# A recommender tower on one core: the beginning reordered, and TensorE's repeated products paced by issued gathers

## What is computed

```python
e = stack([tbl_f[ids[:, f]] for f in range(39)], axis=1)          # (2048, 39, 16)
xk = e
for W, b in ((w0, b0), (w1, b1), (w2, b2)):                       # S = 128 outputs each
    z = relu(einsum('bhd,bkd,hks->bsd', e, xk, W) + b[None, :, None])
    # layers 0 and 1: the first 64 of z are the next xk, the last 64 go out; layer 2: all go out
z = sum over d of the concatenated outputs                        # (2048, 256)
h = relu([z, dense_ctx] @ W_top1 + b_top1); h = relu(h @ W_top2 + b_top2); y = h @ W_top3
```

## Time and profile before

| | us |
|---|---|
| median of 3 runs | 2478.45 (2478.34 to 2480.01) |
| the profiled execution | 2477.58 |
| its span, first to last instruction | 2475.8 |
| TensorE busy in the span | 2422.1 (98%) |
| VectorE busy | 2211.2 (89%) |
| GpSimd busy | 1948.6 (79%) |
| ScalarE busy | 1724.4 (70%) |

### The profile page before, as it was taken

The page is one execution under the profiler, slowest core; times in us unless marked ns, Lnnn a source line. Parts: engine busy times, 40 slices in busy tenths (PEclk is TensorE's granted clock), DMA queues, the critical chain, the costliest instruction groups (busy, mean ns, idle before and its releaser), DMA issues.

```text
span 2475.8 us, 33269 instructions
## 1 busy us (share of the span) xinstructions
PE 2422.1 (98%) x8854; PEld 1640.9 (66%) x8854; DVE 2211.2 (89%) x1876; ACT 1724.4 (70%) x2185; POOL 1948.6 (79%) x1331
## 2 busy tenths in 40 slices
PE   5999999999999999999999999999999999999989
PEld 2566666666666666666666666666666666666655
DVE  1599999999989999999999999899999999999990
ACT  1677777777767777767777776676777777677663
POOL 6688888888878888888888888788888888865550
PEclk9899999999999999999999999999999999999999
DMA  3778667766856766776686677577668667766830
GB/s 74 157 145 175 141 138 160 158 137 141 175 124 139 174 134 140 163 157 137 144 172 138 139 161 160 121 157 160 137 139 174 145 139 154 164 136 134 171 84 0
DMA packets 214716, 352.60 MB, mean 142 GB/s; under 512 B 34382, under 2 KB 47566, under 8 KB 214588
## 3 DMA queue, kind: packets, MB, share of 16 engines
q1 hardware_dynamic: 194717, 347.07, 65.4%
q0 software_dynamic: 19968, 5.15, 2.1%
HBM read 346.97 MB, written 5.12 MB: 142 GB/s over the span
## 4 chain that ended last, share of the span: by engine, by line
PE 54%; POOL 26%; issue 14%; DVE 4%; ACT 1%; POOLq 0%; DMA 0%; ACTq 0%; DVEq 0%
PE ps L858 20%; POOL Pl L397 11%; POOL emb L391 11%; PE ps L868 11%; PE ps L848 10%; PE ps L836 8%; PE ps L831 2%; POOL dir L426 2%; DVE P L731 1%; DVE ps L731 1%; DVE Pl L736 1%; PE ps L983 1%; POOL sqx L403 1%; PE ps L975 1%; PE ps L824 1%
## 5 line engine op out<-in xcount | busy, mean ns | idle before, releaser
L397 POOL TENSOR_TENSOR Pl<-P,Ph 128x1024 fp32r<-128x1024 f32 x448 | 1074.8, 2399 | 285.3 <-ACT Ph L541 261.5
L858 PE MATMUL ps<-Ph,wh 128*128 128x512 f32 x2048 | 965.2, 471 | 9.9 <-ACT Ph L541 9.9
L541 ACT ACTIVATE Ph<-ps 128x1024 fp32r<-128x1024 f32 x576 | 590.3, 1025 | 406.7 <-DVE ps L731 393.0
L731 DVE TENSOR_TENSOR P<-xb,ps 128x1024 f32<-128x1024 f32 x704 | 853.2, 1212 | 2.8 <-DMA xb<-x_dram 2.8
L736 DVE TENSOR_TENSOR Pl<-ps,Ph 128x1024 fp32r<-128x1024 f32 x576 | 705.1, 1224 | 116.1 <-ACT Ph L541 97.4
L858 PE MATMUL ps<-Ph,wl 128*128 128x512 f32 x1920 | 755.5, 393 | 0.0
L868 PE MATMUL ps<-Pl,wh 128*128 128x512 f32 x2048 | 742.2, 443 | 7.4 <-POOL Pl L397 7.4
L391 POOL DMA_INDIRECT emb<-tbl_in,idx x624 | 600.6, 962 | 170.5 <-issue 145.0
L731 DVE TENSOR_TENSOR ps<-xb,ps 128x1024 f32<-128x1024 f32 x576 | 707.1, 1228 | 28.5 <-issue 9.4
L541 ACT ACTIVATE Ph<-P 128x1024 fp32r<-128x1024 f32 x448 | 473.9, 1058 | 186.1 <-DVE P L731 129.8
L868 PEld LDWEIGHTS ps<-Pl,wh 128*128 128x128 f32 x2048 | 384.3, 188 | 200.0 <-issue 118.2
(11 more groups left out here) (68 smaller groups left out, 857.2 us busy)
## 6 DMA issues: line engine op xcount, KB each, us to landing
xb<-x_dram SPq DMA_DIRECT2D x1280, 256.0 KB
emb<-tbl_in,idx POOLq DMA_INDIRECT x624
x_dram<-rows SPq DMA_DIRECT2D x64, 78.0 KB
xb<-w_in SPq DMA_DIRECT2D x16, 128.0 KB
xb<-wt_in SPq DMA_DIRECT2D x2, 512.0 KB, 4.4
xb<-dense_in SPq DMA_DIRECT2D x1, 768.0 KB, 5.3
wp<-w_in SPq DMA_DIRECT2D x4, 128.0 KB
xb<-w0a_in SPq DMA_DIRECT2D x1, 448.0 KB
```

The source lines that it names most:

```text
L397: pool.tensor_tensor(Pl[:, h_slot(ref, c, k)], P[:, p_slot(ref, c, k)], Ph[:, h_slot(ref, c, k)], ALU.subtract).then_inc(low_pool, 1)
L541: act.activation(Ph[:, h_slot(ref, c, k)], p, ACT.Copy).then_inc(rounded, 1)
L731: dve.tensor_tensor(p, xb[:, x], xk.unsqueeze(1).broadcast_to([128, 2, N]), ALU.mult)\
L858: pe.matmul(z_of(c, k), w[:, q, j, :], Ph[:, h_slot(ref, c, k), j, :], start=k in (L1B, L2) and i + j == 0, stop=False)
```

## The change

- DVE: the low halves `wl` of the weights (L702) and the two copies behind them (L711) leave their place ahead of the gathers' end, and stand behind the embedding's low part. What needs them, `transposes(1)` on PE, waits for them (`weights_made` 8). PE's and SP's first waits are for five preparations of weights. `w_st` moves to the end of `xb`, so that the first spreads do not overwrite it.
- The embedding of tile 0 is prepared in two parts: the first four columns d (`D0`) get their high, full and low parts first, and PE's first transposes wait for those alone; the other twelve (`D1`) follow, with their full part on DVE as a `tensor_copy`.
- In the first chunk ACT copies `x2` first and the rows second; PE's first two sums wait for `x2` alone.
- Bias and relu of the lower half (`lower`) of the first chunk's layer 0 and of the last chunk's layer 1 are done by DVE, beside ACT's `direct0` and `direct1`; ACT then copies the result to the upper half.
- The 36 repeated products on PE wait, three at a time, for a count `issued`, which POOL raises after every third gather of tile 0.
- POOL issues 11 gathers of tile 1, not 14, before its first `low`, and 7 behind it.

```diff
--- before.py
+++ after.py
@@ -34,7 +34,7 @@
 
 
 PRE = 4
-WARM = 36
+PACE = 3
 L1B, L2, STEPS = PAIRS - PRE, PAIRS, 2 * PAIRS
 KIND = "GVPVGPVGVPVGVGVGVGVP"
 SPL = [k for k in range(STEPS) if KIND[k] != "P"]
@@ -59,6 +59,7 @@
 SINGLE_STEPS = [k for k in range(STEPS) if TURN[k % PAIRS] == SINGLE // 2]
 assert all(k in SPL for k in SINGLE_STEPS)
 CHUNKS = TILES * CPT
+D0, D1 = slice(0, DC), slice(DC, D)
 NEXT_IDS_AT = (2, 0)
...
@@ -185,6 +186,9 @@
         sel = sel0[0:R2, 0:T0 * R0].rearrange("p (t r) -> p t r", r=R0)
         sel0_st, inc = stage(R2, T0, R0), stage(R0, T0, NF)
         w0a_st, w0b_st = stage(R0, T0, S), stage(R0, T0, S)
+        assert at[0] + NS * 2 * S <= XSLOTS * 2 * N
+        at[0] = XSLOTS * 2 * N - NS * 2 * S
+        assert at[0] >= 2 * PRE * 2 * N
         w_st = stage(128, NS, 2 * S).rearrange("p q (j m) -> p q j m", j=2)
 
         xt = xb[:, :, :, :].rearrange("p q j n -> p (q j) n")
...
@@ -329,8 +338,8 @@
                         .then_inc(xb_in[q], 16)
 
 
-            sp.wait_ge(weights_made, 8)
-            sp.wait_ge(parts_made, 2)
+            sp.wait_ge(weights_made, 5)
+            sp.wait_ge(parts_made, 3)
             write_rows(0, 0)
             for p in range(PRE):
                 spread(0, p)
@@ -434,6 +443,8 @@
             take_ids(0)
             for f in range(NF):
                 gather(f)
+                if f % PACE == PACE - 1:
+                    pool.sem_inc(issued, 1)
 
             def next_ids(T):
 
@@ -442,7 +453,7 @@
                 take_ids(T)
 
             next_ids(1)
-            early, early2 = 14, 18
+            early, early2 = 11, 18
             for f in range(early):
                 gather(f)
             for k in range(L1B, L2):
@@ -556,9 +567,18 @@
                 act.activation(dir1[:, COL1[c % CPT], :], z2_ps, ACT.Relu, bias=bias[:, 2:3]).then_inc(z2_read, 1)
 
 
-            high_emb(0)
-            full_emb(0)
-            copy_x(0, 0)
+            def part(x, d):
+                return x[:, :, d].rearrange("p f d -> p d f")
+
+            act.wait_ge(gathered, 16 * NF)
+            act.activation(emb_h[:, :, D0], emb[:, :, D0], ACT.Copy).then_inc(first_high, 1)
+            act.activation(emb2[:, D0, 0, :], part(emb, D0), ACT.Copy).then_inc(first_full, 1)
+            act.activation(emb_h[:, :, D1], emb[:, :, D1], ACT.Copy).then_inc(emb_high, 1)
+            act.wait_ge(aux_ready, 1)
+            act.activation(x2[:, :], aux_ps[0:R2], ACT.Copy).then_inc(first_x, 1)
+            act.activation(rows_sb, aux_ps[0:NF], ACT.Copy).then_inc(rows_ready, 1)
+            act.wait_ge(rows_ready, 1)
+            act.sem_inc(aux_read, 1)
             square(0, 2, 0, early_ps[0][1])
             rest_squares(0, 0, 1, early_ps[0][0])
             for t in range(1, FULL0):
@@ -566,9 +586,8 @@
             act.wait_ge(squares_done, 1)
             direct0(0)
             act.wait_ge(z0_read, 1)
-            upper(0, z0_ps[:, 0], xk1_upper)
             act.wait_ge(xk1_upper, 1)
-            lower(0, z0_ps[:, 0], xk1_ready)
+            act.activation(z0_ps[hi, 0], z0_ps[lo, 0], ACT.Copy).then_inc(xk1_ready, 1)
 
             act.wait_ge(rows_written, 16)
             copy_x(0, AUX)
@@ -632,9 +651,13 @@
                             direct1(c)
                         if k == RELU1_AT:
                             act.wait_ge(z1_read, T * CPT + c + 1)
-                            upper(1, z1_ps[:, c % 2], xk2_upper)
-                            act.wait_ge(xk2_upper, T * CPT + c + 1)
-                            lower(1, z1_ps[:, c % 2], xk2_ready)
+                            if end:
+                                act.wait_ge(xk2_upper, CHUNKS)
+                                act.activation(z1_ps[hi, c % 2], z1_ps[lo, c % 2], ACT.Copy).then_inc(xk2_ready, 1)
+                            else:
+                                upper(1, z1_ps[:, c % 2], xk2_upper)
+                                act.wait_ge(xk2_upper, T * CPT + c + 1)
+                                lower(1, z1_ps[:, c % 2], xk2_ready)
                         if KIND[k] != "P" and (CPT * ref + c, k) in STEPSET:
                             round_(T, ref, c, k)
                         if end and k == L1B:
@@ -698,17 +721,9 @@
             dve.wait_ge(weights_made, 1)
             dve.tensor_scalar(w0[:, :, :], w0a_st[:, 0:FULL0], 0.5, None, ALU.mult).then_inc(weights_made, 1)
             dve.tensor_scalar(w0b_st[:, FULL0], w0a_st[:, FULL0], 0.5, None, ALU.mult).then_inc(weights_made, 1)
-            dve.wait_ge(parts_made, 2)
-            dve.tensor_tensor(wl[:, :, :, :], w_st, wh[:, :, :, :], ALU.subtract).then_inc(weights_made, 1)
-
             dve.wait_ge(parts_made, 3)
             part = slice(GAP, GAP + REST)
             dve.tensor_tensor(w0x[part, :], w0b_st[part, FULL0], w0x[part, :], ALU.subtract).then_inc(weights_made, 1)
-
-            dve.wait_ge(weights_made, 5)
-            for k in SINGLE_STEPS:
-                q = SPL.index(k)
-                dve.tensor_copy(wh[K1:, q, 1, :], wl[K1:, q, 1, :]).then_inc(weights_made, 1)
 
             dve.wait_ge(incident, 1)
             dve.scalar_tensor_tensor(out=w0[0:NF, 0, :], in0=aux_ps[0:NF, 0:S], scalar=-0.5, in1=w0a_st[0:NF, 0, :],
@@ -742,9 +757,24 @@
                 dve.wait_ge(rest_square, chunk + 1)
                 dve.tensor_tensor(sqx[LOWS, :], rest_sq, sqx[LOWS, :], ALU.subtract).then_inc(rest_ready, 1)
 
+            def lower(layer, z, made):
+                dve.tensor_scalar(z, z, bias[lo, layer:layer + 1], 0.0, ALU.add, ALU.max).then_inc(made, 1)
+
+            def part(x, d):
+                return x[:, :, d].rearrange("p f d -> p d f")
+
+            dve.wait_ge(first_high, 1)
+            dve.tensor_tensor(emb2[:, D0, 1, :], part(emb, D0), part(emb_h, D0), ALU.subtract).then_inc(first_low, 1)
             dve.wait_ge(emb_high, 1)
-            dve.tensor_tensor(emb2[:, :, 1, :], emb[:, :, :].rearrange("p f d -> p d f"),
-                              emb_h[:, :, :].rearrange("p f d -> p d f"), ALU.subtract).then_inc(emb_low, 1)
+            dve.tensor_tensor(emb2[:, D1, 1, :], part(emb, D1), part(emb_h, D1), ALU.subtract).then_inc(emb_low, 1)
+            dve.tensor_copy(emb2[:, D1, 0, :], part(emb, D1)).then_inc(emb_full, 1)
+            dve.wait_ge(parts_made, 2)
+            dve.tensor_tensor(wl[:, :, :, :], w_st, wh[:, :, :, :], ALU.subtract).then_inc(weights_made, 1)
+            dve.wait_ge(weights_made, 6)
+            for k in SINGLE_STEPS:
+                q = SPL.index(k)
+                dve.tensor_copy(wh[K1:, q, 1, :], wl[K1:, q, 1, :]).then_inc(weights_made, 1)
+
             def low_weights():
                 dve.wait_ge(mlp_high, 1)
                 r = slice(2 * GAP, DX)
@@ -755,6 +785,8 @@
                         .then_inc(mlp_low, 1)
 
             rest_low(0)
+            dve.wait_ge(squares_done, 1)
+            lower(0, z0_ps[lo, 0], xk1_upper)
             dve.wait_ge(xk1_ready, 1)
             waiting = None
             for s in range(PRE):
@@ -779,6 +811,9 @@
                                 waiting = None
                             if k == L2 - 1:
                                 low_weights()
+                                dve.wait_ge(plain_done, PLAINS[CHUNKS - 1, L1B - 1])
+                                dve.wait_ge(split_done, SPLITS[CHUNKS - 1, L1B - 1])
+                                lower(1, z1_ps[lo, (CPT - 1) % 2], xk2_upper)
                             continue
                         if k == L1B:
                             dve.wait_ge(xk1_ready, T * CPT + c + 2)
@@ -893,20 +928,31 @@
                 m = pe.matmul(aux_ps[0:NF, 0:S], inc[rows, t, :], w0a_st[rows, t, :], start=t == 0, stop=t == T0 - 1)
             m.then_inc(incident, 1)
 
-            for i in range(WARM):
+            for i in range(PACE, NF):
+                if i % PACE == 0:
+                    pe.wait_ge(issued, i // PACE)
                 pe.matmul(z1_ps[:, 0], wp[:, 0, 0, :], wp[:, 0:2].rearrange("p q j m -> p (q j m)"), start=True, stop=True)
 
 
-            pe.wait_ge(weights_made, 8)
+            pe.wait_ge(weights_made, 5)
             pe.wait_ge(parts_made, 1)
             pe.wait_ge(idx_ready, 2)
-            pe.wait_ge(emb_full, 1)
-            pe.wait_ge(emb_low, 1)
+            pe.wait_ge(first_full, 1)
+            pe.wait_ge(first_low, 1)
             late = None
             for g in range(2):
+                if g:
+                    pe.wait_ge(weights_made, 8)
+                    pe.wait_ge(emb_full, 1)
+                    pe.wait_ge(emb_low, 1)
                 transposes(g)
-                pe.wait_ge(aux_read, READS * g + 1)
+                if g:
+                    pe.wait_ge(aux_read, READS + 1)
+                else:
+                    pe.wait_ge(first_x, 1)
                 for i, t in enumerate((FULL0, 0, 1)):
+                    if i == 2 and not g:
+                        pe.wait_ge(aux_read, 1)
                     sums(t, early_ps[g][i])
```

(5 more changed lines are left out.)

## The result

The changed kernel took 2482.32 us (median of 22 runs, 2478.42 to 2486.76), the kernel before 2478.62 in as many runs beside it: ratio 1.0017, 95% interval 1.0011 to 1.0023. That is no gain but a loss of 3.7 us: less than the 5.0 us (0.2%) that the prediction counted as no change, yet clear of the noise, and far outside the predicted 2467.6 to 2475.3. The profiled execution took 2482.29, its span is 2480.5.

What follows compares the result with a forecast made beforehand. TensorE, busy 98%, was taken as the bound, its start set by the gathers and embedding before about 65 us. Gains 3.34 + 1.28 + 0.61 + 0.68 + 0.67 = 6.6 gave a forecast of 2471.4, range 2467.6 to 2475.3.

Steps and rivals of the forecast that it cites:

- Part 1: Weights' low halves behind tile 0's gathers: the 5.03 gather's stall goes, less 0.55 for increments; net gain 3.34 us.
- The copy was held: POOL's index copy of tile 1 waits for VectorE's subtraction L702 until 64.4; POOL's second subtraction just fits, cost zero.
- Part 2: Between the gathers' landing and the first transposes: preparing a quarter of the embedding first takes 0.90, gaining 1.28 us.
- Part 3: First chunk, x2 copied ahead of the rows: sums start earlier, gain 0.61 us; the later transfers stay hidden.
- Part 4: Lower half on VectorE beside direct0 and direct1: gain 0.68 us in the first chunk, 0.67 in the last.
- The clock: Rival, chance 0.17: shorter TensorE pauses move three steps to full clock, 3 us more gained, 2468.4.
- Part 5: Pacing the 36 repeated products ahead of the first transposes: they end near 54.5, pause about 3.3; priced at 0.
- The slow one: Rival, chance 0.05: each of 12 POOL increments waits for its gather's landing, 1.34 each, 16 in all: 2486.8.
- The stall: Rival, chance 0.05: something else slows the fourteenth gather, which still costs 5.03; part 1 becomes -0.55: 2474.8.
- POOL was not late: Rival, chance 0.09: held copy and slower gathers make POOL's second subtraction 1 to 3 late: 2473.5.

Runs made afterwards that it cites:

- j1: The changed kernel itself, unedited, run again on chip 10 against the kernel before: 2469.75 us, ratio 0.9968.
- j2: The changed kernel without pacing (POOL's increments, TensorE's waits) and with 24 repeated products instead of 36, on chip 10: 2471.25 us, ratio 0.9972.
- h3: The changed kernel without pacing, plus three VectorE operations of 128x1024 at the moved subtraction's old place, on chip 15: 2470.11 us in one run.
- j3: The same kernel as h3, on chip 10 against the kernel before: 2470.82 us, ratio 0.9970.
- i4: The same kernel as h3, timed in several rounds on chip 2 against the kernel before: 2483.27 us, ratio 1.0021.

## Why the prediction was wrong, point by point

The sum itself can be read where the stretch is absent. j1's median is 7.85 under that of before on its chip (2477.6), where 6.6 was forecast (7.1 between medians). The interval of its ratio goes from 4.7 to 10.9 us and holds both.

- *Part 1.* Right in after and j1: the last gather ends at 55.13 and 55.08 for 55.6. The difference is about the increments, priced at 0.55 and free. The copy was held as said, for 4.21 and 4.22 in place of 0.22, and ended at 63.5 and 63.6 (64.4 predicted). The Trainium skill (SBUF — State Buffer, SBUF: two separate sides) says that whichever of the two engines starts first has the shared ports for its whole instruction. Both traces agree: the copy ends 0.08 behind VectorE's subtraction. In j1 POOL stays ahead: its second subtraction is at 89.81 behind 0.56 of idle time, for 90.3 with 0.6 in hand predicted.
- *Part 2.* Copies of 0.33, 0.46, 0.43 for 0.30, 0.44, 0.42. j1's transposes are at 57.49, 5.00 before; 4.62 was the sum.
- *Part 3.* Right in j1: first sums at 58.99, behind x2. The transfers are not quite hidden: VectorE waits for `xb` 1.73, 1.12 and 1.21 between 78 and 86, but TensorE has no idle time there, so nothing is paid.
- *Part 4.* From direct0 to the first product 1.45, for 1.40 predicted and 2.08 before. In the last chunk less: 1.61 in place of 2.08 (0.67 predicted, 0.47 got), since VectorE begins 0.17 behind ScalarE's direct1 there, and its own 0.74 is longer than the direct1 (0.68) that I had hidden it behind. The copy takes 0.57, where I had taken 0.65. TensorE's wait behind this place fell from 4.61 to 4.13. In after's timeline:

```profile
2393.42 0.68 ACT L564 ACTIVATE dir<-ps,bias 64x512 f32<-64x512 f32 x1 [1.96 <-PE ps L903]
2393.59 0.74 DVE L761 TENSOR_SCALAR ps<-ps,bias 64x512 f32<-64x512 f32 x1
2394.43 0.57 ACT L656 ACTIVATE ps<-ps 64x512 f32<-64x512 f32 x1 [0.32 <-DVE ps L761]
2395.03 1.23 DVE L746 TENSOR_TENSOR ps<-xb,ps 128x1024 f32<-128x1024 f32 x1 [0.70 <-ACT ps L656]
```

- *The clock.* In j1 it went the better way in part: half for 6.9 and 6.8 us at the first chunks, where before it was half for 13.7 and 10.2. The edges follow from the means in j1's busy time by stretch (0.97 over 53 to 58 is a fall at 57.7, 0.68 over 73 to 78 one at 74.8):

```profile
53.00:58.00 5.00, 1.82 (x8) 0.65 (x6) 0.68 (x2) 1.18 (x3) 1.77 (x2) 0.97 0.06 5
58.00:63.00 5.00, 4.05 (x8) 1.86 (x7) 5.00 (x3) 3.20 (x6) 3.62 (x1) 0.50 0.08 19
63.00:68.00 5.00, 5.00 (x13) 2.24 (x12) 1.56 (x4) 2.39 (x4) 3.55 (x4) 0.84 0.98 234
...
73.00:78.00 5.00, 3.45 (x7) 1.85 (x8) 4.90 (x6) 3.98 (x7) 3.82 (x4) 0.68 0.31 86
78.00:83.00 5.00, 5.00 (x14) 3.42 (x13) 2.16 (x3) 1.18 (x2) 4.51 (x4) 0.64 1.07 220
```

  From transposes to first product j1 needs 13.33, before 15.25: 1.92 less. Parts 3 and 4 were priced at 1.29 of it; the other 0.6 I put down to the clock, as what is left. So the first product is 6.9 earlier, not 5.9.
- *Part 5 is the step that failed.* I wrote that the repeated products end "near 54.5" and that a pause of 3.3 then stands ahead of the transposes. j1 has it so: its products end at 54.3 and the pause is 3.18. In after they end at 73.5, and the transposes, which I had started the moment the embedding was ready, wait behind them in TensorE's stream until 73.36. That is 15.9 later than in j1. At the first product 13.7 of it are left, and between the medians, each against before beside it, 11.55. I had counted the products as free because TensorE idled behind them. They were free only as long as each took 0.86: 72 records of work that nobody reads stood ahead of the critical instruction, and a slack of 3.3 was all the margin. The only price that I had put on them was what they do to the clock; none of my rivals let TensorE's own stream be late. The increments were not understood either: the twelfth group was to wait for the 36th gather, issued at 51.9, but all 13 increments had passed by 40.2. Why the records fell to one per 1.40 stays open.
- *The rivals.* The slow one (increments that wait for gathers) did not happen: increments cost nothing. The stall did not stay, and POOL was not late. The loss in the first comparison has another mechanism, that none of my cases held. Nothing in the profile of before shows it; what could be read there was how much stood to be delayed. That the forecast fits j1 so well is in part luck: free increments and the better clock gave more than the sum, and part 4 in the last chunk less.

## What to carry to other kernels

Work that only keeps an engine's clock up stands in the same queue as the work that the end waits for: give it an end well before that work can start, not 3 us before. Eighteen and 24 products kept a gain (0.9970 to 0.9979; of these only the 18 on a chip with the stretch), where 36 lost it on three of the five chips seen by number. j1's 0.9968 is not clear of j2's 0.9972 on the same chip, so that nothing measurable is to be had from more of them. And before an "absent" in one run is put down to the edit, run the kernel that has the effect on the same chip: h3's reading fell for want of that.

## What the runs showed of the hardware

- In the runs on chips 7, 11 and 2 TensorE passed its records 1.40 us apart, beginning between 40 and 46 and ending near 60, in a long run of one product, while gathers (1.25 apart) and the copies of ScalarE and VectorE kept their pace. The same file ran them 0.43 apart on chips 15 and 10 and had the stretch on chip 2 (h3, j3, i4).
- A semaphore increment on POOL took 17 ns, and the last of them passed some twelve gathers ahead of the gather it stands behind; "issued", counted in this way, is known long before the gather begins to run.
- A copy of 128x39 on POOL (0.22 in the earlier trace rows) took 4.21 beside VectorE's subtraction with two operands in memory, and a gather took 5.03 beside it. Beside h3's three VectorE operations of 128x1024 with one operand in memory (3.48 together) no gather took over 0.95.
